# A one-layer decoder with routed experts: the cross-attention mask moved into the stacked score operands, the self stacks laid in two row halves, the expert weights loaded for each tile

## What is computed

```python
x = x + self_attention(layernorm(x))            # q, k, v, softmax over 128 keys, projection, no mask
scores = einsum('bhqd,bhkd->bhqk', q, k) / sqrt(8)          # cross-attention, 77 keys
scores = where(mask[:, None, :, :] == 0, -1e9, scores)      # one mask for all 16 heads
x = x + (softmax(scores) @ v) @ Wo.T + bo
# experts: E = 8, F = 512, each token goes to its 2 best of 8
gate = l2norm(h @ Wp.T) @ l2norm(sim).T / temperature       # h = layernorm(x)
out = x + sum over the token's 2 experts of p * (gelu(h @ W1[e] + b1[e]) @ W2[e] + b2[e])
```

## Time and profile before

| what | value |
|---|---|
| median of 3 runs (lowest to highest) | 1165.42 us (1161.81 to 1165.63) |
| the profiled execution, its own time | 1154.14 us |
| its span, first to last instruction | 1152.4 us |
| mean granted TensorE clock | 0.953 of 2.4 GHz |
| busy: PE, PEld, DVE, ACT, POOL | 86%, 66%, 65%, 70%, 52% of the span |
| moved by DMA | 144.06 MB, mean 125 GB/s |
| matmuls | 11621 |

### The profile page before, as it was taken

How to read it: one execution, slowest core, us unless ns; L and a number is a source line. 1 busy time by engine, 2 the same in 40 slices (tenths; PEclk the granted TensorE clock), 3 DMA queues, 4 the chain that set the end, 5 groups by cost and what they waited for, 6 DMA issues and landing times.

```text
span 1152.4 us, 31418 instructions
## 1 busy us (share of the span) xinstructions
PE 992.5 (86%) x11621; PEld 760.0 (66%) x11621; DVE 748.2 (65%) x2099; ACT 802.7 (70%) x1652; POOL 603.0 (52%) x825
## 2 busy tenths in 40 slices
PE   2467889999999999999999999899889999999900
PEld 1255667777777777777777777576657678888800
DVE  2654655666676666666666667356648988888816
ACT  2144466777777777777777777667779899999900
POOL 4313332446555556546546554445557666666750
PEclk9966999999999999999999999999999999999955
DMA  3336674635644745565456343464112354332229
GB/s 89 80 88 146 159 165 92 164 97 145 176 108 119 181 116 130 136 146 147 115 145 163 105 122 103 104 192 111 53 43 69 92 172 126 120 100 76 66 69 371
DMA packets 109313, 144.06 MB, mean 125 GB/s; under 512 B 23117, under 2 KB 87456, under 8 KB 104360
## 3 DMA queue, kind: packets, MB, share of 16 engines
q1 hardware_dynamic: 97816, 120.25, 40.5%
q0 software_dynamic: 9168, 17.21, 4.8%
q10 hardware_dynamic: 2176, 4.59, 1.1%
HBM read 88.30 MB, written 55.36 MB: 125 GB/s over the span
## 4 chain that ended last, share of the span: by engine, by line
PE 68%; DVE 8%; DMA 6%; issue 5%; ACT 5%; SPq 4%; POOL 3%; DVEq 0%; POOLq 0%; ACTq 0%
PE pv L1610 10%; PE sc_a L1591 9%; PE sc_m L1575 8%; PE wb L1565 5%; PE wb L1559 5%; PE sc_a L1596 5%; PE wb L1554 4%; PE sc_m L1580 3%; PE pv L1838 2%; PE pv L1831 2%; PE pv L1832 2%; DMA big<-y_d 2%; DVE negm_m L1084 2%; PE wb L1776 2%; PE wb L1645 1%
## 5 line engine op out<-in xcount | busy, mean ns | idle before, releaser
L839 ACT ACTIVATE probs<-sc_a 77x512 f32<-77x512 f32 (+1 forms) x512 | 300.6, 592 | 139.5 <-PE sc_a L1596 86.2
L1084 DVE TENSOR_REDUCE negm_m<-sc_m 128x4 f32<-128x512 f32 x256 | 169.7, 683 | 76.8 <-PE sc_m L1575 76.1
L633 POOL DMA_INDIRECT y_d<-yo,row x156 | 165.8, 1063 | 90.3 <-issue 38.9
L1084 DVE TENSOR_REDUCE negm_cm<-sc_m 128x4 f32<-128x308 f32 x256 | 119.3, 472 | 132.4 <-PE sc_m L1580 132.1
L624 POOL DMA_INDIRECT xs_d<-xrow,slot_i x128 | 133.4, 1042 | 98.6 <-PE sc_a L1596 51.7
L1610 PE MATMUL pv<-probs,big 128*32 128x128 f32 x4096 | 165.5, 280 | 0.6
L1575 PE MATMUL sc_m<-kbig,qbig 96*128 96x128 bf16 x1024 | 104.2, 228 | 35.9 <-DMA kbig<-stk_k 14.0
L1610 PEld LDWEIGHTS pv<-probs,big 128*32 128x32 f32 x4096 | 96.1, 109 | 55.3 <-ACT probs L839 26.7
L1287 DVE TENSOR_TENSOR gl<-g,gh 128x512 fp32r<-128x512 f32 x156 | 107.1, 689 | 35.7 <-ACT g L987 35.4
L1575 PEld LDWEIGHTS sc_m<-kbig,qbig 96*128 96x128 bf16 x1024 | 70.8, 101 | 80.3 <-issue 53.0
L1591 PE MATMUL sc_a<-qbig,kbig 102*128 102x128 bf16 x1024 | 100.7, 222 | 1.2 <-ACT probs L839 1.2
(11 more groups left out here) (218 smaller groups left out, 2388.8 us busy)
## 6 DMA issues: line engine op xcount, KB each, us to landing
xg<-xs_d SPq DMA_DIRECT2D x39, 260.0 KB, 2.7
stk_q<-parts_q SPq DMA_DIRECT2D x16, 384.0 KB, 2.9
stk_k<-parts_k SPq DMA_DIRECT2D x16, 384.0 KB, 2.6
qbig<-stk_q SPq DMA_DIRECT2D x16, 384.0 KB
kbig<-stk_k SPq DMA_DIRECT2D x32, 192.0 KB
stk_cq<-parts_cq SPq DMA_DIRECT2D x16, 384.0 KB, 2.9
cbig<-stk_cq SPq DMA_DIRECT2D x16, 384.0 KB
xin<-x_dram SPq DMA_DIRECT2D x16, 256.0 KB
```

What stands on the lines that cost most here:

```text
L633: nc.gpsimd.indirect_dma_start(out=y12_d, in_=yo[i % NY][:, c, :], in_offset=None, bounds_check=2 * B * S - 1, oob_is_err=False, out_offse ...
L839: nc.scalar.activation(probs[e % 4][0:rows], sc_a[e % 2][0:rows], ACT.Exp, scale=scale)\
L1084: nc.vector.tensor_reduce(out=negm[n][:, s, HG * g + 4 * half:HG * g + 4 * half + 4], in_=sc_m[u % 2][:, 0:4 * cols].rearrange("p (j k) -> ...
```

## The change

**Cross mask.** The mask comes transposed from the host (77 keys in the partitions). POOL forms `mbT` (77 x 512, one buffer). DVE copies it to all 16 heads of the cross-q stack `cqs`, rows 0 to 76, in 4 copies of 4 heads, in units 3, 4, 9 and 10 of the self half (`MASKS`). In the cross-k stack rows 0 to 76 hold an identity for each head, written once by POOL's `places`. The 48 rows of parts stand behind them and 3 rows for the maxima last: 128 rows. L1580 and L1596 are gone. The cross stacks now have a slot for each of the 16 heads in q as well, and no zero rows, so ck is stacked by 3 DMAs, not 6.

**Self stacks.** Group g = 0 of the heads lies in rows 0 to 50, group 1 in rows 64 to 114, for q and k alike; the zero rows (and POOL's `zeros`) are gone. `scores` and `shifted` multiply 48 and 51 rows, from row 0 or from row 64. q is stacked by 6 DMAs, not 3.

**Experts.** W1, W2 and the biases of an expert lie in one row of 1032 numbers per partition in DRAM. `load(i)` brings 528 KB for each tile, three buffers in turn, and needs the splits of tile `i-3` to be done. `weights` and the table reads in `split_w` and `split_v` are gone.

**POOL.** The mask operation stands ahead of `third("cq", t)`, not behind it.

```diff
+GP = 64
+KM = GP + KS + 3
+CS = SC + KS
+CR = CS + 3
+WROW = FC * D + F + 8
+NW = 3
+MASKS = (3, 4, 9, 10)
...
+                    for g in range(NG):
+                        if n == "k" and b < 2:
+                            sp.wait_ge(ident_ok.sem, 7)
+                            ones_under(n, dst, GP * g + KS, slice(0, HG))
+                        for place, skip in RUNS:
+                            left = 3 - skip
+                            some = slice(0, left) if n == "q" else slice(skip, 3)
+                            row, view = GP * g + DH * place, stk[n][some].rearrange("c (i g j) t -> g (c i) j t", i=DH, g=NG)
+                            sp.dma_start(dst[row:row + DH * left, :, :], view[g]).then_inc(stacked[n].sem, 16)
...
+                        row, view = SC + DH * place, stk[n][some].rearrange("c (i h) t -> (c i) h t", i=DH)
+                        sp.dma_start(dst[row:row + DH * left, :, :], view).then_inc(stacked[n].sem, 16)
...
+                    if i >= NW:
+                        sp.wait_ge(bias_ok.sem, bias_ok.val(i - NW))
+                        sp.wait_ge(wl_ok.sem, wl_ok.val(i - NW))
+                        sp.wait_ge(vl_ok.sem, vl_ok.val(i - NW))
+                    e = sp.value_load(tab[0:1, 0, bass.ds(i, 1)], min_val=0, max_val=E - 1)
+                    sp.dma_start(wraw[i % NW], W12[bass.ds(e, 1)].rearrange("e p w -> p (e w)")).then_inc(w_in[i % NW].sem, 16)
                     if i >= 2:
                         sp.wait_ge(xT_f.sem, xT_f.val(i - 2))
                         sp.wait_ge(read.sem, read.val(i - 2))
...
-                        third("cq", t)
-                        wait_block(pool, st_f["c"], t - 2)
+                        wait_block(pool, mask_ok, t - 1)
                         pool.wait_ge(mk_in.sem, mk_in.val(t))
                         pool.nop(nofuse=True)
-                        nc.gpsimd.tensor_scalar(out=mbias[par][:], in0=mk[:], scalar1=0.0, scalar2=MASKED,
-                                                op0=ALU.is_equal, op1=ALU.mult).then_inc(mb_ok.sem, 1)
...
+                        nc.gpsimd.tensor_scalar(out=mbT[:].rearrange("k (s p) -> k s p", s=NS), in0=mk[:], scalar1=0.0,
+                                                scalar2=MASKED, op0=ALU.is_equal, op1=ALU.mult).then_inc(mb_ok.sem, 1)
+                        third("cq", t)
...
+                def masks(b, dst, k):
+
+                    if k == 0:
+                        dve.wait_ge(mb_ok.sem, mb_ok.val(b))
+                        wait_block(dve, st_f["c"], b - 2)
+                        dve.nop(nofuse=True)
+                    n = H // len(MASKS)
+                    nc.vector.tensor_copy(dst[0:SC, k * n:(k + 1) * n, :], mbT[:].unsqueeze(1).broadcast_to([SC, n, T]))\
+                        .then_inc(mask_ok.sem, 1)
...
+                def operands(n, half, g, shift):
+
+                    if n in ("m", "s"):
+                        return slice(GP * g, GP * g + KS + 3 * shift), 4 * half
+                    return slice(0, CR if shift else CS), HG * g + 4 * half
...
-                    if bias:
-                        i = nc.tensor.matmul(sc_m[u % 2][:, 0:4 * cols], identb[:],
-                                             bias[:, s, :].unsqueeze(1).broadcast_to([128, 4, cols]),
-                                             start=False, stop=True, skip_group_check=True)
...
-                        pe.wait_ge(mb_ok.sem, mb_ok.val(t - 1))
-                        maxi = ("cm", t - 1, cqs[1 - par], cks[1 - par], SC, mbias[1 - par])
+                            pe.wait_ge(preset["ck"].sem, t)
+                        pe.wait_ge(mask_ok.sem, mask_ok.val(t - 1))
+                        maxi = ("cm", t - 1, cqs[1 - par], cks[1 - par], SC)
```

More of the change, by code:

```diff
@@ L179, in program, with stacks @@
         rest["ck"] = sa("rest_ck", [128, TC])
-        def stacks(tile, at, heads):
-            n = (H if heads == H else HG)
-            cols = {H: TC, HG: T}[heads]
-            return [tile[0:KM, at + i * n * cols:at + (i + 1) * n * cols].rearrange("p (h t) -> p h t", h=n) for i in range(2)]
-        ks = [kbig[0:KM, i * H * T:(i + 1) * H * T].rearrange("p (h t) -> p h t", h=H) for i in range(2)]
-        qs = stacks(qbig, 0, HG)
-        cks, cqs = stacks(cbig, 0, H), stacks(cbig, 2 * H * TC, HG)
+        def stacks(tile, at, rows, heads, cols):
+            return [tile[0:rows, at + i * heads * cols:at + (i + 1) * heads * cols].rearrange("p (h t) -> p h t", h=heads)
+                    for i in range(2)]
+        qs, ks = stacks(qkbig, 0, KM, HG, T), stacks(qkbig, 2 * HG * T, KM, HG, T)
+        cks, cqs = stacks(cbig, 0, CR, H, TC), stacks(cbig, 2 * H * TC, CR, H, T)
         negm = {n: sa(f"negm_{n}", [128, NS, H]) for n in ("m", "cm")}
@@ L293, in program @@
         tab_ok, table_step, iotas, base_seen = sem("tab_ok"), sem("table_step"), sem("iotas"), sem("base_seen")
-        w_in, fill_st = sem("w_in", 16), sem("fill_st", 16)
+        w_in, fill_st = [sem(f"w_in{i}", 16) for i in range(NW)], sem("fill_st", 16)
         def follow(old, per):
@@ L402, in stack @@
                     for place, skip in RUNS:
                         left = 3 - skip
[L404 to L411 removed]
+                        some = slice(0, left) if n == "cq" else slice(skip, 3)
@@ L1589, in shifted @@
                         pe.wait_ge(exp_ok[n].sem, exp_ok[n].val(b, u - 1))
+                    rows, slot = operands(n, half, g, True)
                     for j in range(4):
                         i = nc.tensor.matmul(sc_a[u % 2][0:cols, j * S:(j + 1) * S],
-                                             kst[:, HG * g + 4 * half + j, s * cols:(s + 1) * cols],
-                                             qst[:, 4 * half + j, s * S:(s + 1) * S],
-                                             start=(j == 0 or not bias), stop=not bias, skip_group_check=bool(bias))
-                    if bias:
-                        i = nc.tensor.matmul(sc_a[u % 2][0:cols, :], bias[:, s, :],
-                                             identb[:].unsqueeze(1).broadcast_to([128, 4, S]),
-                                             start=False, stop=True, skip_group_check=True)
+                                             kst[rows, slot + j, s * cols:(s + 1) * cols], qst[rows, slot + j, s * S:(s + 1) * S],
+                                             start=True, stop=True)
                     i.then_inc(st_f[n].sem, 1)
```

147 lines of the change are left out of this document (60 added, 87 removed).

## The result

The changed kernel takes 1191.78 us (median of 4 runs, 1187.27 to 1199.09); the kernel before, on the same chip, 1165.28 us (4 runs). The ratio is 1.024, with a 95% interval of 1.0185 to 1.0296: slower by 26.5 us, where 49 us less were forecast.

The account below looks back on a forecast made before the run. PE was taken to bound the kernel, fully busy in the cross half. -60 (mask matmuls) + 5 (copies) + 3 (self stacks) + 3 (weights) = -49 us on 1165.4 gave 1116 us, range 1085 to 1144.

Parts of the forecast that it names:

- the transfers, not the issues, set the landing: Cross half: q in six pieces shifts the `mscr` landing by 0.5 us, between 0 and 1.6, as bytes stay the same.
- bound (19.6 us): Cross half: the `mscr` transfer lands 19.1 us after its start, plus 0.5 us for q's issues.
- with slack: 0: Steady step: the ck stack saves three SP issues, which have slack, so it counts 0 us.
- rival E: Cross half: `mscr` landing moves to 23 us with SP's longer list, saving 0.8 us, not 4.0; 1158 us, chance 0.03.
- Mask matmuls, -60: Cross halves: without two mask matmuls a unit, 19.8 us in place of 23.8; -60 us, bounds 27 to 88.
- Copies, +5: Self halves: four DVE mask copies of 1.2 us, mostly hidden in DVE's waits; +5 us, bounds 0 and 67.
- Rivals B and C: Self-half copies: B, thinner cover, 1130 to 1144 us, chance 0.14; C, 2.3 us a copy, 1178 us, chance 0.04.
- Self stacks, +3: Program start: six q pieces add 2.9 us of issue, twice; transfers hide about half; +3 us.
- No time on PE: Self halves: the self-stack matmuls have as many columns as before, so they cost PE nothing.
- Rival A: Self half: products of the two row halves overlap, 14 us; with more cross gain 1065 to 1100 us; chance 0.23.
- Weights, +3: Expert tiles: per-tile loads cost nothing except one PE wait at tile 15; +3 us, bounds 2 and 5.
- Rival D: Expert tiles: DMA engines give only 150 GB/s, so weights starve the tiles; +74 us, 1190 us; chance 0.05.

Follow-up runs that it names:

- x_spread: The changed kernel with each stack request, self and cross, writing every second partition in place of neighbouring ones; ratio 0.9853 to the kernel before.
- b_nomask: The kernel before with the mask matmuls left out of both cross score products and nothing put in their place; ratio 0.9629.
- b_weights: The kernel before with the expert weights loaded per tile and nothing else changed; ratio 1.0065, 7.6 us slower.

## Why the prediction was wrong

The step that failed is the one sentence "the transfers, not the issues, set the landing", with the same bytes taken to mean the same landing. The first half was right, and issues did get cheaper (1.25 us for the three of the ck stack, where the six of before took 4.55). But the rate was read from one stretch of before and taken as the engines' own, while it belonged to rows that k's slices spread by two. The diff took that slice away (`row + g:row + H * left:NG`), and I costed bytes and counted requests, and never the partitions. Place: 45 us of the miss, shown by `x_spread`.

The second failure is a wait I did not price: only `mscr`'s trip had a bound (19.6 us), `cmscr`'s had none, and "with slack: 0" stood for the stacks ahead of it. It is the one PE waits for at 12 of 13 borders. The trace of before had its landing 2.5 us ahead of the cross half on average; its dump now takes 4.8 us longer to come back (9.3 against 4.5), and 4.8 - 2.5 = 2.3 us is what PE waits at a border (29 us in 13, 2.2 on average). With the rows spread the trip is 1.9 us longer than before, less than the slack, and the waits are gone but for 1.7 us once and those of the fill. It is the longer trip that used the slack up, not the shorter half: in `b_nomask` the cross halves are 3 us shorter and the landing is as far ahead as before. With the rows spread, moving 564 KB out of its way was still worth 18 us, and 5 us before the change: 13 us of the miss, by difference of ratios (two sets, so 3 to 23 us). This was rival E in kind, a landing that ends the half. But E had the other landing, a cause that did not come (the length of SP's list), and a price that could at most take the gain, since it left out the fill and the clock.

*Mask matmuls, -60:* mis-sized. They are worth 43 us alone (17 us of the miss). PE's busy time fell by 4.7 us a half (23.77 to 19.03), not 5.6; over eleven steps the cross half fell by 3.1 us on average, to 20.6, not by 4.0, and the self half grew by 0.25, which was not in the sum. So a unit's two mask matmuls cost PE 0.30 us (4.74 / 16) and not the 0.35 that I read from the chain, and in what is left PE waits between the units, longest for DVE. The transfers had no part in this.

*Copies, +5:* right in size (4.5), by wrong terms: they take 0.68 us, not 1.2, and what POOL adds is 0.7 us a step, not 2.4. That the sum came out is luck, within an interval of 0 to 12 us. Rivals B and C did not come.

*Self stacks, +3:* the sign of the whole was hidden by the place: 10 us slower as changed, 2.6 us faster when spread. "No time on PE" left out that they save some. Rival A's mechanism came in full: the products of the two row halves do run side by side, and PE's busy time in a self half falls by 1.5 us, more than the 0.9 us that A counted. Its price did not come: of the 14 us it gave, 2.6 are seen (0.2 to 5), so most of what PE saves doesn't reach the end of the self half.

*Weights, +3:* 7.6 us. The wait was right in `b_weights`, the clock behind it and about 2 us whose place stays open were not in it. Rival D did not come.

The sum of the measured terms: -43 (matmuls) + 4.5 (copies) + 7.6 (weights) - 2.6 (halves, spread) + 13 (what the loads' order gives beyond before) + 45 (place) = +24.5 us, against +26.5 measured. Each term is uncertain by 2 to 10 us and the sum by some 14 us, so an agreement to 2 us is partly luck. The 45 us are also the measured change less `x_spread`, so what is tested is only that the other five, -20.5 us, give the 17 us by which `x_spread` beats the kernel before. That the terms simply add is argued, not shown.

## What to carry to other kernels

When a change rewrites the slice that a DMA fills, compare the partitions of one request, before and after, as carefully as its bytes: rows that are neighbours share a way in, and spreading them by a step of two cost nothing here, where the row order is free, as in a contraction. A busy DMA share with a low GB/s beside it is how this looks in a profile; read both. And when PE has work taken off it, price every landing at the borders that its time covered, the one behind the other stacks too; read from the trace of before how far ahead of its reader each one lands, and set against it by how much its trip can grow. A wait can cost nearly its own length again by the clock that falls behind it; here the clock fell behind 9 of the 12.

## What the hardware showed that I had not expected

16 rows of 8192 bytes take 994 ns a packet into neighbouring partitions and 401 ns at step 2; 16384 bytes 2408 and 1254. The dump of 48 KB on another engine's queue was as late (8.4 us) as on the same one (9.3). Products of 48 and 51 rows in the two halves of the array start 10 ns apart. A bfloat16 copy of 0.68 us took up to 2.42 us when a POOL operation was running at its start. And the clock: 1.0 in the 4.4 us in which PE was idle for half of the time, then 0.53 for 3.6 us of full work behind it.
